# Attention block: q, k and v products split into f16 high and low halves, with DVE and ACT lists reordered

## The reference

```python
xi = _gn(x) + emb_W[coalition]              # normalised image plus an agent's embedding
q, k, v = xi @ Wq + bq, xi @ Wk + bk, xi @ Wv + bv
scores = q @ k.T / sqrt(16)                 # 8 heads of 16 channels, 16 x 16 agents
attn = softmax(where(mask[s], scores, NEG)) # five masks s
out = mean_s(attn[s] @ v) @ Wo + bo
x = x + out
```

## Time and profile before

| | |
|---|---|
| three runs, median (lowest to highest) | 1130.23 us (1130.2 to 1131.82) |
| the profiled execution | 1129.39 us, of which the span from first to last instruction is 1127.6 us |
| busy in the span | PE 972.8, DVE 835.6, ACT 668.5, POOL 550.3 us |
| set-up and statistics | 0 to 42 us |
| attention, filling (passes 0 to 2) | 42 to 82 us |
| attention, passes 3 to 15 | 82 to 335 us |
| attention, emptying | 335 to 371 us |
| token mixer, then the experts | 371 to 1127.6 us |

### The profile page before, as it was taken

The page is one execution under the profiler, slowest core; times in us unless marked ns, Lnnn a source line. Parts: engine busy times, 40 slices in busy tenths (PEclk is TensorE's granted clock), DMA queues, the critical chain, the costliest instruction groups (busy, mean ns, idle before and its releaser), DMA issues. The chain is left out here.

```text
span 1127.6 us, 39936 instructions
## 1 busy us (share of the span) xinstructions
PE 972.8 (86%) x14086; PEld 825.6 (73%) x14086; DVE 835.6 (74%) x2058; ACT 668.5 (59%) x1348; POOL 550.3 (49%) x588
## 2 busy tenths in 40 slices
PE   4799999899997689788888886249999999999996
PEld 3478777788776345576766765249999999999995
DVE  4687777677776334778888888428888888888885
ACT  1176756566573325777676674137777676767763
POOL 0327474565647621455655655504444444444444
PEclk9899999999999777889999998559999999999998
DMA  9011010111100300112122122557766667666660
GB/s 331 20 40 40 22 32 29 31 31 31 35 20 3 112 19 19 39 51 65 59 67 68 58 65 73 89 147 268 253 237 238 239 241 251 240 239 242 236 226 33
DMA packets 87697, 127.95 MB, mean 113 GB/s; under 512 B 12436, under 2 KB 53555, under 8 KB 87533
## 3 DMA queue, kind: packets, MB, share of 16 engines
q1 hardware_dynamic: 75116, 107.08, 28.0%
q0 software_dynamic: 9120, 17.15, 4.8%
q10 hardware_dynamic: 3298, 1.37, 0.8%
HBM read 31.61 MB, written 20.91 MB: 47 GB/s over the span
## 5 line engine op out<-in xcount | busy, mean ns | idle before, releaser
L1353 POOL DMA_INDIRECT out<-e_y,e_xg x156 | 155.8, 999 | 66.7 <-issue 66.7
L258 POOL TENSOR_SCALAR vm<-v,early 128x512 f32<-128x512 f32 x96 | 148.9, 1568 | 0.0
L824 POOL DMA_INDIRECT rows<-m_rows,m_place x128 | 126.1, 985 | 40.1 <-issue 40.1
L1408 PE MATMUL e_ps<-e_xt,weights 128*128 128x128 f16 x624 | 137.7, 221 | 8.3 <-DMA e_fed<-weights 4.2
L1410 PE MATMUL e_ps<-e_xt,weights 128*128 128x128 f16 x624 | 137.8, 221 | 0.0
L1409 PE MATMUL e_ps<-e_xt,weights 128*128 128x128 f16 x624 | 137.5, 220 | 0.0
L1408 PE MATMUL e_ps<-e_xt,e_fed 128*128 128x128 f16 x624 | 137.5, 220 | 0.0
L1409 PE MATMUL e_ps<-e_xt,e_fed 128*128 128x128 f16 x624 | 137.4, 220 | 0.0
L1410 PE MATMUL e_ps<-e_xt,e_fed 128*128 128x128 f16 x624 | 137.4, 220 | 0.0
L1498 DVE SCALAR_TENSOR_TENSOR e_hid_hl<-e_hid,e_hid_hl 128x512 f16<-128x512 f32 x156 | 108.1, 693 | 17.2 <-ACT e_hid_hl L1471 16.6
L1492 DVE SCALAR_TENSOR_TENSOR e_hid<-e_ps,e_act 128x512 f32<-128x512 f32 x156 | 106.9, 685 | 10.7 <-PE e_ps L1410 9.4
(11 more groups left out here) (262 smaller groups left out, 3082.3 us busy)
## 6 DMA issues: line engine op xcount, KB each, us to landing
e_fed<-weights SPq DMA_DIRECT2D x156, 416.0 KB
e_xg<-rows SPq DMA_DIRECT2D x156, 66.5 KB, 2.3
resid<-in_x SPq DMA_DIRECT2D x8, 1024.0 KB, 14.3
xb<-in_x SPq DMA_DIRECT2D x32, 256.0 KB, 2.6
m_rows<-resid SPq DMA_DIRECT2D x32, 256.0 KB, 2.8
out<-e_y,e_xg POOLq DMA_INDIRECT x156, 3.1
m_w_f<-in_L_ffn_gate_up_proj SPq DMA_DIRECT2D x1, 2048.0 KB, 8.4
rows<-m_rows,m_place POOLq DMA_INDIRECT x128, 2.4
```

The source lines that it names most:

```text
L258: ins = g.tensor_scalar(vm[:, u, :, n, :], full, pair_of[:, n:n + 1], None, ALU.mult)
L824: g.indirect_dma_start(rows_dram, bass.IndirectOffsetOnAxis(ap=place[:, slot, j:j + 1], axis=0), rows[:, slot, j, :], None).then_inc(s.row ...
L1353: nc.gpsimd.indirect_dma_start(out_rows, bass.IndirectOffsetOnAxis(ap=who, axis=0), y[:, slot, i, :], None, bounds_check=B * TOK - 1, oob_ ...
L1408: t.matmul(o, hi, x2[0], start=True, stop=False)
```

## The change

After the set-up constants, DVE scales the three weight matrices by 64 into `w_big`, ACT rounds them to f16 (`w_hl[:, 0]`), and DVE stores the rest, also in f16 (`w_hl[:, 1]`). In each pass ACT rounds `xi u` to f16 (`x_high u`), DVE stores the rest (`x_low u`), and every product is three f16 products added in PSUM: high x high, low x high and high x low. PE's products wait for `x_low` in place of `xi`. The factor 64 is taken out again when q, k and v are copied out of PSUM. In DVE's list xi 1 stands ahead of p 1; it stood behind it.

```diff
+            def x_high(k, ring, u):                       # ACT
+                b = 2 * k + u
+                need(act, s.xi_done, b + 1)
+                a.activation(xi_hl[:, u, 0], xi[:, u, :], ACT.Copy).then_inc(s.xh_done, 1)
...
+            act.wait_ge(s.w_big_done, 1)
+            a.activation(w_hl[:, 0], w_big[:], ACT.Copy).then_inc(s.wh_done, 1)
...
-                (1, exp, 0), (3, o, 0), (3, o, 1), (1, et, 0), (1, exp, 1), (1, et, 1), (0, v, 0), (3, ot, 0),
+                (1, exp, 0), (3, o, 0), (0, x_high, 0), (3, o, 1), (1, et, 0), (1, exp, 1), (0, x_high, 1), (1, et, 1), (0, v, 0), (3, ot, 0),
...
-                need(pe, s.xi_done, b + 1)
+                need(pe, s.xl_done, b + 1)
...
-                t.matmul(bank_q, w_f[:, 0, :], xi[:, u, :], start=True, stop=True).then_inc(s.q_psum, 1)
+                hi, lo = (xi_hl[:, u, l, :] for l in range(2))
+                t.matmul(bank_q, w_hl[:, 0, 0, :], hi, start=True, stop=False)
+                t.matmul(bank_q, w_hl[:, 0, 0, :], lo, start=False, stop=False)
+                t.matmul(bank_q, w_hl[:, 1, 0, :], hi, start=False, stop=True).then_inc(s.q_psum, 1)
...
-                    last = t.matmul(bank_vo[:, j * P:(j + 1) * P], xi[:, u, j * P:(j + 1) * P], w_f[:, 2, :], start=True, stop=True)
+                    t.matmul(o, hi, w_hl[:, 0, 2, :], start=True, stop=False)
+                    t.matmul(o, hi, w_hl[:, 1, 2, :], start=False, stop=False)
+                    last = t.matmul(o, lo, w_hl[:, 0, 2, :], start=False, stop=True)
...
+            v.tensor_scalar(split[:], cst[:, CONST["parity"][0]:CONST["parity"][0] + 6], 1.0 / WS, None, ALU.mult).then_inc(s.split_done, 1)
+            v.tensor_scalar(w_big[:], w_f[:, 0:3, :], WS, None, ALU.mult).then_inc(s.w_big_done, 1)
+            dve.wait_ge(s.wh_done, 1)
+            v.tensor_tensor(w_hl[:, 1], w_big[:], w_hl[:, 0], ALU.subtract).then_inc(s.wl_done, 1)
...
+            def x_low(k, ring, u):                        # DVE
+                b = 2 * k + u
+                need(dve, s.xh_done, b + 1)
+                v.tensor_tensor(xi_hl[:, u, 1], xi[:, u, :], xi_hl[:, u, 0], ALU.subtract).then_inc(s.xl_done, 1)
...
-                (1, shifted, 0), (0, shifts), (0, xi_, 0), (2, p, 0), (1, shifted, 1), (2, p, 1), (0, xi_, 1), (0, even_queries),
+                (1, shifted, 0), (0, shifts), (0, xi_, 0), (2, p, 0), (0, x_low, 0), (1, shifted, 1), (0, xi_, 1), (2, p, 1), (0, x_low, 1), (0, even_queries),
```

More of the change, by code:

```diff
@@ L193, in agent_attention @@
         xi = sb("xi", [P, 2, TOK])
+        xi_hl = sb("xi_hl", [P, 2, 2, TOK], F16)
+        w_big = sb("w_big", [P, 3, C])
+        w_hl = sb("w_hl", [P, 2, 3, C], F16)
+        split = sb("split", [P, 6])
         qm = sb("qm", [P, 2, T, 2, A])
@@ L211, in agent_attention @@
             setup_v spread_psum spread_done half_set setup_pe gT_psum gst_done gvar_done gsum_done gmean_psum rstd_done
-            xT_psum xi_done q_psum k_psum v_psum q0_done q1_done km_done v32_done vm_done
+            split_done w_big_done wh_done wl_done xh_done xl_done xT_psum xi_done q_psum k_psum v_psum q0_done q1_done km_done v32_done vm_done
             s_psum rmax_done sm_done e_done et_psum et_done d_psum recip_done w_psum pm_done
@@ L283, in odd_queries @@
                     ins = a.activation(qm[:, 1, :, r, :], bank_q.rearrange("p (t a) -> p t a", a=A), ACT.Identity,
-                                       bias=bq_par[:, r:r + 1], scale=parity[:, r:r + 1])
+                                       bias=bq_par[:, r:r + 1], scale=split[:, r:r + 1])
                 ins.then_inc(s.q1_done, 1)
@@ L293, in keys @@
                     ins = a.activation(km[:, u, :, n, :], bank_k.rearrange("p (t a) -> p t a", a=A), ACT.Identity,
-                                       bias=bk_pair[:, n:n + 1], scale=pair_of[:, n:n + 1])
+                                       bias=bk_pair[:, n:n + 1], scale=split[:, 2 + n:3 + n])
                 ins.then_inc(s.km_done, 1)
@@ L300, in v @@
                 need(act, s.vm_done, b - 5)
-                a.activation(v32[:, slot, :], bank_vo, ACT.Copy).then_inc(s.v32_done, 1)
+                a.activation(v32[:, slot, :], bank_vo, ACT.Copy, scale=1.0 / WS).then_inc(s.v32_done, 1)
             def o(k, ring, u):
@@ L329, in _ @@
             ins.then_inc(s.spread_done, 1)
+            act.wait_ge(s.split_done, 1)
             pipelined(act, PAIRS, 4, 6, [
-                (1, exp, 0), (3, o, 0), (3, o, 1), (1, et, 0), (1, exp, 1), (1, et, 1), (0, v, 0), (3, ot, 0),
+                (1, exp, 0), (3, o, 0), (0, x_high, 0), (3, o, 1), (1, et, 0), (1, exp, 1), (0, x_high, 1), (1, et, 1), (0, v, 0), (3, ot, 0),
                 (0, keys, 0), (3, ot, 1), (0, v, 1), (0, odd_queries), (0, keys, 1),
@@ L366, in _ @@
             pe.wait_ge(s.spread_done, 1)
+            pe.wait_ge(s.wl_done, 1)
             pe.wait_ge(s.gst_done, B + 1)
@@ L397, in q_k @@
                     need(pe, s.q1_done, k)
-                t.matmul(bank_q, w_f[:, 0, :], xi[:, u, :], start=True, stop=True).then_inc(s.q_psum, 1)
+                hi, lo = (xi_hl[:, u, l, :] for l in range(2))
+                t.matmul(bank_q, w_hl[:, 0, 0, :], hi, start=True, stop=False)
+                t.matmul(bank_q, w_hl[:, 0, 0, :], lo, start=False, stop=False)
+                t.matmul(bank_q, w_hl[:, 1, 0, :], hi, start=False, stop=True).then_inc(s.q_psum, 1)
                 need(pe, s.km_done, b)
-                t.matmul(bank_k, w_f[:, 1, :], xi[:, u, :], start=True, stop=True).then_inc(s.k_psum, 1)
+                t.matmul(bank_k, w_hl[:, 0, 1, :], hi, start=True, stop=False)
+                t.matmul(bank_k, w_hl[:, 0, 1, :], lo, start=False, stop=False)
+                t.matmul(bank_k, w_hl[:, 1, 1, :], hi, start=False, stop=True).then_inc(s.k_psum, 1)
             def v(k, ring, u):
                 b = 2 * k + u
-                need(pe, s.xi_done, b + 1)
+                need(pe, s.xl_done, b + 1)
                 need(pe, s.v32_done, b)
@@ L407, in v @@
                 for j in range(TILES):
-                    last = t.matmul(bank_vo[:, j * P:(j + 1) * P], xi[:, u, j * P:(j + 1) * P], w_f[:, 2, :], start=True, stop=True)
+                    o = bank_vo[:, j * P:(j + 1) * P]
+                    hi, lo = (xi_hl[:, u, l, j * P:(j + 1) * P] for l in range(2))
+                    t.matmul(o, hi, w_hl[:, 0, 2, :], start=True, stop=False)
+                    t.matmul(o, hi, w_hl[:, 1, 2, :], start=False, stop=False)
+                    last = t.matmul(o, lo, w_hl[:, 0, 2, :], start=False, stop=True)
                 last.then_inc(s.v_psum, 1)
@@ L572, in even_queries @@
                 for r in range(2):
-                    ins = v.tensor_scalar(qm[:, 0, :, r, :], bank_q.rearrange("p (t a) -> p t a", a=A), parity[:, r:r + 1],
+                    ins = v.tensor_scalar(qm[:, 0, :, r, :], bank_q.rearrange("p (t a) -> p t a", a=A), split[:, r:r + 1],
                                           bq_par[:, r:r + 1], ALU.mult, ALU.add)
```

## The result

The changed kernel takes 1152.98 us (median of 4 runs, 1152.31 to 1154.34) where the kernel before took 1131.03 (4 runs, 1130.2 to 1134.23): ratio 1.0204, 95% interval [1.018, 1.0228]. The profiled execution took 1153.64 us with a span of 1151.8, 24.2 more than before.

A forecast was written before the change was run, and what follows sets the result against it. PE was taken to bound the stage, at 18.89 us a pass; 14.8 us for the passes, 1.8 set-up and 2.0 filling add 18.6 to 1129.39, forecast 1148 us, with an 8-in-10 range of 1138 to 1161.

The forecast's parts named there:

- set-up: New split, w_big and rounding instructions ahead of DVE's bn_stats, paid in full: +1.8 us, between 1.2 and 2.3.
- filling: Passes 0 and 1, where x_high and x_low lie bare: +2 us for both, between +0.5 and +3.5.
- The wait before ot 0: PE from xT 1 to ot 0: pt copy waits for p 1, now behind xi 1; 1.82 becomes 3.64 us.
- The second obstacle: Rival before ot 0: the copy waits for x_high 1, not p 1; +0.08 us a pass, 1134 us, 6%.
- PE's products: Shorter f16 products on PE: q_k 0 and q_k 1 0.37 us less each, v 0.22 each, about 1.18 a pass.
- its first rival: PE's saving is all there is, with p 1 ending before PE's et 1 as before: 1111 us, 4%.
- x_low 0: New on DVE between p 0 and shifted 1, slowed 0.4 us beside POOL's L258: costs PE about 0.2 us a pass.
- the sign of being wrong: In the changed profile, x_low lasting 0.69 us everywhere would take 3 us off the forecast.
- Sum of a pass: Passes 2 to 15: the product savings, the ot 0 wait and x_low 0 give +1.06 us each, +14.8 in all.
- the step that costed the new wait at its length alone: PE's wait between xT 1 and ot 0, counted as 1.82 us more a pass.
- The waits for instructions: PE's "issue" waits, 5.1 us in four places before pv, may go or double: +-5 us.
- The rival built on that rule: x_low 0 on DVE is shut out by POOL twice: 1.7 us a pass in place of 0.2, 1169 us, 10%.

The follow-up runs named there:

- in f32 alone: The kernel before, f32 products and no split, with xi 1 put ahead of p 1 on DVE and nothing else changed: ratio 1.0259.
- the kernel with the added products: The kernel after, with 11 f16 products of 128x384 put between v 0 and ot 0 on PE from pass 2 on: ratio 1.0156.

## Why the prediction was right, and where its sizes were off

The direction and the mechanism were right: 1148 us, slower, because p 1 now stands behind xi 1 and holds the pt copy, and with it ot 0. The measured 1153 lies in the range, but not for the range's reasons: its upper part was meant for an x_low that POOL holds, which did not come, and the clock, which did, took its place. That part is luck. The span grew by 24.2 us and not by 18.6; by places:

| | predicted | measured |
|---|---|---|
| set-up (first xT on PE, 43.02 to 45.21) | 1.8 | 2.2 |
| filling, to the first qk of pass 3 (82.12 to 87.49) | 2.0 + 1.06 | 3.2 |
| passes 3 to 15 (253.29 to 272.79) | 13 x 1.06 = 13.8 | 19.5 |
| behind them | 0 | -0.7 |

- *The wait before ot 0*: 1.82 to 3.64 predicted, 3.69 measured, and in f32 alone 20.6 us a pass. Every step of the chain fits: p 1 at S + 1.46 (267.97 - 266.51; predicted 1.47), the copy at S + 2.95 (2.90). The price of the order is also shown by taking it away: 1.0204 to 1.0061.
- *The second obstacle*, x_high 1, was foreseen as a rival's mechanism, with ot 0 at S + 2.86 if it alone held the copy. That is the kernel with p 1 ahead: +0.12 us a pass (18.84 - 18.72; predicted +0.08). Behind p 1 it is hidden, which is why moving it alone does nothing.
- *PE's products*: q_k 1.30 (1.34 predicted), v 0.67 (0.67), q_k 1 with its gap 1.39 (1.45). With both obstacles gone a pass is 0.99 us shorter. For v 0 the prediction has a saving of 0.22 in its sum of PE's products and 0.27 in its first rival; either lies inside the wait.
- *x_low 0*: the +0.2 was wrong; it costs nothing, which is nearly the sign of being wrong that the prediction priced at 3 us off. It started at once and took 0.68 us in every pass from 2 on but the one behind the jump (0.80). The L555 from which it was priced began 0.10 us behind the start of its L258 (58.45 - 58.35), x_low 0 begins 1.2 us behind one (below).
- *Sum of a pass*: without x_low 0 the prediction's terms give +0.86, and at full clock it is 19.53 - 18.72 = +0.81 (a common pass of the kernel with the added products, and of the kernel before). Thirteen passes are then 10.5 of the 19.5 us.
- *What failed*: the step that costed the new wait at its length alone. I had written of the clock for the filling and the token mixer, not for the passes between. Of the other 9.0 us, 3.8 lie in the pass of the jump, which grew from 22.4 to 27.0, 0.8 of it by the order, and has 6.8 us at 1.2 GHz; 5.2 lie in the rest, about what seven stretches at 0.66 to 0.90 us a pass come to (20.19 to 20.43 against 19.53). The waits for instructions, for which the prediction allowed +-5 us, I can't separate from this in the passes in which both occur. Without loops there are fewer such waits, and the sizes come out alike: passes 3 to 15 grew by 265.90 - 245.74 = 20.2 us, of which 13 x 0.81 = 10.5 are the sum of a pass, and the other 9.6 come near what twelve stretches at 20.50 - 19.53 = 0.97 us give, 11.6.

The added bn_stats delay is 2.03 us (21.50 to 23.53): 1.5 for the new instructions from 22.03 on, and 0.53 that was already there before the first of them. In pass 0 PE's first product is 49.46 - 45.97 = 3.49 late, of which 2.19 is the set-up and 1.30 x_high and x_low lying bare (1.4 predicted).

What decides in which passes the clock falls stays open. In the pass shown first (ot 0 at 270.20) PE had waited just as long and the clock stayed full; there, as in four of the five others whose ot 0 no fall followed, it had also lost half a microsecond or more to waits for instructions earlier in the pass; but in the pass behind the jump the clock fell in spite of such a wait. In the f32 kernel with the order changed, with waits of 1.8 us, it fell three times between 90 and 360 us. The runs show that the falls behind ot 0 go when the idling goes, and that each costs 0.66 to 1.1 us; they do not show what decides whether it comes.

## What to carry to other kernels

An instruction that stands early on its engine because its input is there early should stay ahead of one that waits for another engine, above all if a third engine reuses its buffer. Work out the moment of each release from the start of the instruction waited for, obstacle by obstacle, since the second stands hidden behind the first. And cost a new wait of PE by its length and by the clock behind it.

The order with p 1 ahead and x_high 1 behind the copy turns the change into a gain: 0.9942, and 0.9904 without loops, where the kernel before without loops has 0.9957.

## What the runs showed of the chip

*POOL beside DVE.* Here POOL's L262 runs three times for each image, 1.56 us each when nothing lies beside it; the rows show the two that meet the window asked for. x_low 0 starts 1.2 us behind the start of the second one (302.85), x_low 1 0.40 us behind it (308.71). The timelines of POOL, at two places, and of DVE in the same pass:

```profile
301.30 3.10 POOL L262 TENSOR_SCALAR vm<-v,early 128x512 f32<-128x512 f32 x2
...
307.16 3.10 POOL L262 TENSOR_SCALAR vm<-v,early 128x512 f32<-128x512 f32 x2
```

```profile
304.05 0.68 DVE L597 TENSOR_TENSOR xi_hl<-xi,xi_hl 128x512 f16<-128x512 f32 x1
...
309.10 0.82 DVE L597 TENSOR_TENSOR xi_hl<-xi,xi_hl 128x512 f16<-128x512 f32 x1
```

x_low 1 is longer by 0.14 us, and in the passes where it starts 0.23 to 0.25 behind an L262, it takes 0.98 to 1.00; from 0.7 on it is not longer. So it was held to about half a microsecond into the L262, and ended at 309.92, before that one did (310.26). The Trainium skill, "SBUF — State Buffer", section "Who interferes with whom", has the second instruction blocked until the first has finished; no x_low here was. The rival built on that rule, 1169 us, is refuted.

*Jumps.* Behind the jump of its loop DVE stood 3.3 us and PE 1.83 and 1.33 us with no releaser, and written out these waits were gone. The Trainium skill, "Runtime: NRT & Kernel Launch", section "Instruction fetch mechanics", says that a taken branch out of the part that is loaded forces a fetch before the engine can go on; the traces agree with it as far as they go: they show the waits behind the jumps, not which part was loaded. Written-out lists are not free of such waits: PE still waited 2.8 us before pv in three places with all four lists written out:

```profile
PE ps L476 <- issue: 2.8, 3, 1.2
```
